# Six local-attention layers written out, with another order of work in each round, other PSUM banks, and another entry to the 8-head attention

## What is computed

```python
x = x + tanh(g_xattn[0]) * L0_xattn(ln(x), ctx)   # 16 heads, keys from 77 context rows
x = x + tanh(g_ffn[0])   * L0_ffn(ln(x), ...)     # six local layers
x = x + tanh(g_xattn[1]) * L1_xattn(ln(x), ctx)   # 8 heads
x = x + tanh(g_ffn[1])   * L1_ffn(ln(x))          # mixture of 8 experts
...                                               # two more pairs

def L0_ffn(x):
    for i in range(6):
        x = attn_layer(shift_tokens(x), Wqkv[i], q_scale[i], k_scale[i], Wo[i]) + x
        x = ffn_layer(shift_tokens(x), ln_g[i], ln_b[i], W1[i], b1[i], W2[i], b2[i]) + x
    return x
```

## Time and profile before

| | us |
|---|---|
| three runs | 2498.87, 2504.11, 2506.43 |
| median | 2504.11 |
| the profiled execution's own time | 2502.32 |
| its span, first to last instruction | 2500.4 |
| mean granted TensorE clock | 0.981 of full |

### The profile page before, as it was taken

The page is one execution under the profiler, slowest core; times in us unless marked ns, Lnnn a source line. Parts: engine busy times, 40 slices in busy tenths (PEclk is TensorE's granted clock), DMA queues, the critical chain, the costliest instruction groups (busy, mean ns, idle before and its releaser), DMA issues. The chain is left out here.

```text
span 2500.4 us, 84963 instructions
## 1 busy us (share of the span) xinstructions
PE 2379.8 (95%) x32650; PEld 1666.1 (67%) x32650; DVE 1861.0 (74%) x4616; ACT 1770.3 (71%) x3859; POOL 1662.9 (67%) x2011
## 2 busy tenths in 40 slices
PE   8889999999999999999999999999889898999898
PEld 6746666566666666566666666666468777999567
DVE  6768887888878887788778878888387776555574
ACT  5668888888878887888878888888653375332555
POOL 5668888888888887788888888888341164000562
PEclk9989999999999999999999999999999998999899
DMA  3011111121111111221121112111350000000022
GB/s 132 2 36 41 34 33 37 48 52 46 32 48 50 47 36 33 55 54 36 34 55 44 48 36 53 33 32 37 89 172 1 1 2 1 1 0 1 20 68 84
DMA packets 98410, 104.07 MB, mean 42 GB/s; under 512 B 34873, under 2 KB 60548, under 8 KB 97540
## 3 DMA queue, kind: packets, MB, share of 16 engines
q1 hardware_dynamic: 98180, 100.93, 15.2%
HBM read 41.31 MB, written 6.09 MB: 19 GB/s over the span
## 5 line engine op out<-in xcount | busy, mean ns | idle before, releaser
L1261 ACT ACTIVATE area<-ps 64x128 f32<-64x128 f32 (+7 forms) x1480 | 747.0, 530 | 201.2 <-PE ps L860 64.8
L1761 POOL TENSOR_TENSOR area<-area 128x512 f32<-128x512 f32 x384 | 485.7, 1275 | 128.5 <-DVE area L2239 120.9
L1776 POOL TENSOR_TENSOR area<-area,rnq 128x512 f32<-128x512 f32 x384 | 397.2, 1045 | 15.3 <-ACT rnq L1434 8.3
L870 PE MATMUL ps<-lw,area 128*128 128x512 f32 x768 | 375.4, 611 | 4.5 <-DVE area L2239 3.2
L898 PE MATMUL ps<-lw,area 128*64 128x512 f32 x1536 | 373.0, 606 | 0.1
L2237 DVE TENSOR_TENSOR area<-ps,table 128x512 f32<-128x512 f32 x384 | 261.3, 681 | 16.9 <-ACT area L1398 16.8
L2219 DVE TENSOR_REDUCE ssq<-area 128x8 f32<-128x512 f32 x384 | 259.6, 676 | 2.1 <-ACT area L1398 2.1
L2239 DVE TENSOR_TENSOR area<-ps,table 128x512 f32<-128x512 f32 x384 | 259.9, 677 | 0.0
L887 PE MATMUL ps<-ident,area 128*128 128x128 f32 x1536 | 237.7, 278 | 5.0 <-POOL area L1776 4.8
L1398 ACT ACTIVATE area<-ps 128x512 f32<-128x512 f32 x384 | 216.8, 590 | 29.3 <-PE ps L870 29.2
L887 PEld LDWEIGHTS ps<-ident,area 128*128 128x128 f32 x1536 | 178.7, 141 | 78.3 <-issue 57.0
(11 more groups left out here) (290 smaller groups left out, 4950.9 us busy)
## 6 DMA issues: line engine op xcount, KB each, us to landing
area<-area SPq DMA_DIRECT2D x768, 64.0 KB, 2.0
lw<-in_wqk SPq DMA_DIRECT2D x24, 256.0 KB
area<-in_moe_w SPq DMA_DIRECT2D x24, 256.0 KB, 2.8
area<-product_rows SPq DMA_DIRECT2D x16, 256.0 KB
moe_gu<-in_wvT SPq DMA_DIRECT2D x12, 256.0 KB, 3.0
moe_gu<-in_wout SPq DMA_DIRECT2D x12, 256.0 KB, 3.0
area<-area SPq DMA_DIRECT2D x96, 31.8 KB
product_rows<-lw SPq DMA_DIRECT2D x7, 308.0 KB
```

What stands on the lines that cost most here:

```text
L870: nc.tensor.matmul(banks[:, lb_qk[j], :], xsT[s], wqk[w.p][:, j * 512:(j + 1) * 512], start=True, stop=True).then_inc(l_qk_ps, 1)
L1261: return nc.scalar.activation(dst, src, ACT.Identity if kw else ACT.Copy, **kw)
L1761: pool.tensor_tensor(QR[s][:, cols], QR[s][:, cols], RA[s][:, cols], ALU.add).then_inc(l_rsum, 1)
L1776: pool.tensor_tensor(rows, rows, rnq[s][:, 8 * j:8 * j + 8, None].to_broadcast([S, 8, LD]), ALU.mult).then_inc(l_qkn, 1)
```

## The change

1. The loops of the local layers are written out in every engine's queue.
2. Each engine has another order in `stages`, with the waits that this order needs; SyncE issues a unit's transfers one letter earlier.
3. The PSUM banks of the passes are others.
4. SyncE's wait for the output weights comes at round 0 and that for the old layer at round 4 of a layer; weights are loaded from round 0 on.
5. `context_weights` is moved ahead of the wait for the last residual (PE) and ahead of the norming into `Y` (ACT).
6. At the end, five groups of value rows are made inside the last two rounds (three, then two) instead of four behind the last but one and one later.
7. In the 8-head attention all layer norms are made in quads ahead of the rounds, into `Y`; the first round (without scores) goes; keys and value rows move by a round; other banks; row groups are read back in three parts (4, 4 and 8 sequences); the wait for all value rows moves from the first scores to the first transpose of probabilities.

Core of the diff, the order of each engine's `stages` shown as it is after:

```diff
-        lb_tokens, lb_qk, lb_qkT, lb_v = 7, (6, 2, 2, 4), (4, 0, 3, 6), (6, 7, 1, 5)
-        lb_scores, lb_probs = ((4, 5), (0, 1)), (0, 6)
-        lb_att, lb_xnT, lb_up, lb_down = 0, 1, (3, 7), 5
-        lb_wvo = (1, 3)
+        lb_tokens, lb_qk, lb_qkT, lb_v = 1, (2, 3, 1, 4), (4, 7, 3, 5), (5, 6, 7, 0)
+        lb_scores, lb_probs = ((3, 4), (6, 7)), (7, 6)
+        lb_att, lb_xnT, lb_up, lb_down = 7, 1, (5, 6), 0
+        lb_wvo = (0, 2)
...
-                with engine.Fori(2, IT - 1) as pr:
+                for pr in range(2, IT - 1):
...
-            with engine.Fori(0, DEPTH // 2 - 1) as lp:
+            for lp in range(DEPTH // 2 - 1):
```

SyncE:

```diff
-                if c: middle_values0(*c)
-                if d: shifted_tokens(*d)
-                if c: middle_values1(*c, edge=edge)
+                if b: middle_values0(*b)
+                if c: shifted_tokens(*c)
+                if b: middle_values1(*b)
...
-                    if n == 3:
+                    if n == 0:
                         sp.wait_ge(l_wvo_ps, 2 * (2 * lp + p + 1))
+                    if n == 4:
                         sp.wait_ge(ffn_done, G + (2 * lp + p) * B)
-                    if 3 <= n < 3 + len(parts):
+                    if n < len(parts):
...
             for i, (lo, hi) in enumerate(RAW):
                 sp.wait_ge(v_ready, 16 + i + 1)
                 rows_to_memory(lo, hi)
+                if i == 2:
+                    sp.wait_ge(rows_out, 16 * FIRST_PIECES)
+                    rows_from_memory(0, 4, rows_in[0])
                 if i == 4:
                     sp.wait_ge(rows_out, 16 * PIECES)
-                    rows_from_memory(0)
+                    rows_from_memory(4, 8, rows_in[1])
```

VectorE, before and after:

```diff
-                if c: first_residual(*c)
                 if a: tokens(*a)
-                if b:
-                    masked(*b, 0)
-                    maxima(*b, 0)
+                if d:
+                    hidden(*d, 0)
+                    hidden(*d, 2)
                 if c:
                     shifted_stats(*c)
                     statistics(*c)
-                if a: rotated(*a, 2)
+                if d: hidden(*d, 1)
+                if a: rotated(*a, 0)
+                if b:
+                    masked(*b, 0)
+                    maxima(*b, 0)
+                    masked(*b, 1)
+                if c: norm_shift(*c)
+                if b: maxima(*b, 1)
+                if a: rotated(*a, 2)
                 if b:
                     sums(*b, 0)
...
                 if d: second_residual(*d, edge=edge)
+                if b: first_residual(*b)
```

Before the local layers and in the attention:

```diff
             strip_attention(XA[0], 0)          (PE)
             pe.wait_ge(w1_loaded, 112)
+            pe.wait_ge(sc_masked, 2 * B)
+            context_weights()
             pe.wait_ge(x_updated, G + LNY)
-            context_weights()
...
             strip_attention(XA[0], 0)          (ACT)
+            context_weights()
             for q in range(QUADS):
                 act.wait_ge(r_shift, q + 1)
                 for c in (2, 3):
                     last = copy(Y[:, q * 4 + c, :], X[:, q * 4 + c, :], scale=RSQ[q][:, c:c + 1], bias=VEQ[q][:, c:c + 1])
                 last.then_inc(x_updated, 2)
             act.wait_ge(v_ones, 4)
-            context_weights()
             for half in range(2):
                 values_outputs(0, 0, half)
```

More of the change, by code:

```diff
@@ L529, in local_transformer @@
             for n in range(B, B + 3):
-                stages(*(layer_unit(1, DEPTH // 2 - 1, n - k) if n - k < B else None for k in range(4)))
-                if drain and n == B + 1: drain()
+                last = tuple(layer_unit(1, DEPTH // 2 - 1, n - k) if n - k < B else None for k in range(4))
+                if drain and n > B:
+                    stages(*last, drained=n - B)
+                else:
+                    stages(*last)
         block = ctx.enter_context(nc.Block())
@@ L708, in first_value_rows, with second_value_rows @@
             def first_value_rows():
-                for i in range(4):
+                for i in range(3):
+                    value_rows(i)
+            def second_value_rows():
+                for i in (3, 4):
                     value_rows(i)
@@ L1038, in quad_T @@
+                if b:
+                    probs_T(*b, 0, ahead=a)
+                    probs_T(*b, 1, ahead=a)
+                if d: down(*d, 1, edge=edge)
+                if c: up(*c, 0)
+                if b:
+                    probs_values(*b, 0)
+                    probs_values(*b, 1)
+                if a: queries_keys_T(*a, 0)
             def quad_T(m, q, banks):
@@ L1245, in _ @@
             pe.wait_ge(t_prep, 1)
[L1246 removed]
+            local_transformer(pe, stages, fresh=True, drain=True)
             attention(XA[1])
```

447 lines of the change are left out of this document (220 added, 227 removed).

## The result

The changed kernel takes 2550.39 us (median of 2545.11, 2549.26, 2551.52 and 2554.05) against 2505.21 for the kernel before: ratio 1.0184, 95% interval 1.0158 to 1.021. It is slower by 45 us, where 2498, a little faster than before, was forecast. The profiled execution took 2545.11, its span 2543.3.

The account below looks back on a forecast made before the run. TensorE hardly rests now; in the new order a loop through VectorE, the shift transfer and GpSimd sets the round. Local layers -8, their entry +3, attention entry -1: -6 on 2502.3 gives 2496; forecast 2498 (median 1.8 higher), range 2446 to 2526.

Parts of the forecast that it names:

- the walk of the new order: Local layers: operation times summed along one round, from the statistics' start to the next, giving 16.73 us a round.
- The loop and its 3.6 us for the shift: Local layers: residual, shift transfer (3.6 us), statistics, rotation, mask and probabilities close a chain that sets the round at 16.73.
- the signs named for it: Local layers: statistics wait for DMA 1 to 2 us a round, TensorE for the mask about 0.4, rounds alternate by 0.3.
- the signs of being wrong: Local layers: rounds of 16.2 with no wait for the mask, or rounds above 17 with waits for GpSimd's probabilities.
- The floor rules: Rival, chance 0.22: the loop is shorter than summed, local-layer rounds fall to 16.2 to 16.4, whole 2446 to 2465.
- The probabilities come later still: Rival, chance 0.26: ScalarE's exponentials or VectorE's reciprocal delay GpSimd's second probabilities in each local-layer round; 0.3 counts, whole 2527.
- Loops and SyncE's wait: Local layers: written-out loops remove 4.1 us once, inner turns nothing; the moved wait removes five disturbances of about 2.5 us.
- Nothing for the longer code: Local layers: written-out loops were charged 0 us for instruction fetches, as queues run ahead of TensorE.
- the third rival: Chance 0.05: the change gives only its removals, the order being neutral; 4 and 12 us go, +2 stays, whole 2490.
- GpSimd's table: Local layers: the next layer's table, six small operations between the two probabilities, lengthens the loop by 5 x 1.4, +7 us.
- Entry of the local layers: Before the first rounds: context-weight copies ahead of ScalarE's normed blocks make the first query product 3 us later; bounds 0, +4.
- Entry of the 8-head attention: After the local layers: keys start 8.7 us earlier, but TensorE waits for group 5's copy; net -1, bounds -9 and +4.

## Why the prediction was wrong, point by point

**The step that failed** is in the walk of the new order: "the second mask follows at 3.30, the shift of the norm at 3.90, the second maximum at 4.02". It gives the shift of the norm 0.1 us. Measured are masks at 1.93 and 3.25 after the statistics, the shift of the norm at 3.85, and the maximum at 4.67. The duration is that of the steady rounds of the kernel before, in which GpSimd was idle or began in nearly the same instant; in the new order GpSimd's differences are running in 95 of 96 rounds when it begins, and in 94 it lasts until they end. The price is 0.69 in a steady round and 0.62 on the average of the local layers, in place of nothing: with 96 rounds 60 us, against a miss of 52. All behind it (probabilities ready at 9.24, found 9.90) is late by this alone.

**The round.** With that operation made short, nothing else changed, the round is 16.65 (forecast 16.73), alternating by 0.3 as forecast, with the statistics waiting for the transfer and TensorE waiting some 0.17 and 0.46 in turn for the mask (23.4 in all); the whole came to 2490 (forecast 2498). The loop and its 3.6 us for the shift (3.75 and 3.45 in turn in the kernel after) were right. So were the signs named for it in the kernel after: waits for the mask (24.4 in 71 times) and for the DMA. And of the signs of being wrong, "rounds above 17 with waits for GpSimd's probabilities" came.

That this run is within 8 us of the forecast is in part luck. Its local layers, measured as in the earlier trace rows, take 1614 (forecast 1619). From the last token transpose to the mixture it is 3.0 more than before, where 1 less was forecast, and the unchanged stages after it are 3.7 shorter, which no term had.

**The rivals.** *The floor rules* needs a shorter loop, which is what the run with GpSimd's order changed has: its floor is 16.36 and not 16.15, since TensorE's pieces summed fell 0.2 short. *The probabilities come later still* had the right place (TensorE waits 19.9 us for them) and the right sign, but its cause was ScalarE's exponential or a reciprocal, half a microsecond at most; both had slack. Its 2527 lies under the result. The range left no room for an operation that itself becomes longer.

**Loops and SyncE's wait.** 4.1 for the turn: 4.2. Nothing for the inner loops, from a wrong reading of the earlier trace rows: 3.6. 5 x 2.5 for the wait: four times, 10.5 together. Nothing for the longer code: TensorE shows 4.4 us of new idle issue in seven places (L937), which is the most that it can have cost; the order of before, written out, does not show it. Both removals were right and are part of the kernel after. The sum of 96 new rounds did not contain them, only the third rival did, so their sizes did not move the forecast. They hide what the new order cost: with both removals the local layers take 1592 in the old order and 1656 in the new one, 64 more, of which the long operation is 59.

**GpSimd's table.** 5 x 1.4 on the chain was forecast; moved away it gave 1.4 or 1.5 a round and 8.7 in all.

**Entry of the local layers.** +3, bounds 0 and +4: in the kernel after the first query product is 5.8 later (139.03 and 133.27), in the four runs with the same entry 3.4 to 5.8; 2.4 is thus the spread between executions of the same code. By the fourth token transpose the five stand at 181.7 to 184.6, where four kernels with the order of before stand at 181.2 to 182.7. So three have made up all of it; the kernel after and one other are still some 2.2 late. The place itself costs 1.6 at the entry and nothing later, as its two runs show. ScalarE's timeline in the kernel after, where the copies of the earlier trace rows now stand ahead of the normed blocks:

```profile
127.61 2.06 ACT L1285 ACTIVATE w<-ps 128x512 f32<-128x512 f32 x4 [10.73 <-PE ps L698]
129.54 3.18 ACT L1285 ACTIVATE Y<-X,m_lg 128x128 f32<-128x128 f32 x8
```

**Entry of the 8-head attention.** The mechanism was right: the value rows stand in the waits before, and TensorE waits behind them for the copy of group 5, 7.06 us (forecast 8 to 10). TensorE's timeline in the kernel after, as in the earlier trace rows:

```profile
1827.00 5.32 PE L714 MATMUL ps<-w,ctxT 128*128 128x512 f32 x12
...
1841.11 6.93 PE L729 MATMUL ps<-ctxT,w 128*128 128x462 f32 x16 [0.60 <-ACT lw L1285]
...
1857.78 2.07 PE L714 MATMUL ps<-w,ctxT 128*128 128x512 f32 x2 [7.06 <-ACT lw L1285]
```

From the last token transpose to the first keys it is 48.8 instead of 52.8, 4 of the 8.7 us; from there to the mixture the gain is gone: 144.8 in all, 142.7 before. -1 was forecast with bounds -9 and +4; +2 came, though the granted clock of this stretch moves it by as much: 142.7 at 0.95 in the kernel before, 138.7 at 0.99 with its loops and wait mended.

## What to carry to other kernels

Before a VectorE operation is moved, ask what GpSimd does at its new place. In these kernels the operation with two tensors from SBUF lasted until the end of the GpSimd operation that had begun shortly before it, and this shows as a longer operation and in no list of waits. For each group of instructions, read the longest duration beside the median: one of eight times the median, in rounds of one kind, is a price that a new order may charge in every round. Where it bites, there are two ways out that worked here: one operand as a pointer scalar, or the operation in GpSimd's pause. One tensor instead of two is no safe rule, as `floors` in the next section shows. And in an order that TensorE nearly fills, check GpSimd's order and VectorE's together.

## What the runs showed of the hardware

**A lock, by who is first.** In 95 of 96 rounds of the kernel after, differences were running when the operation began, as a rule for 0.16 us, and it took 0.90 (median). In the kernel before, 31 of them began 1 to 10 ns behind a GpSimd operation of 1.05 us and took 0.15 all the same; the five that began 76 to 81 ns behind one took 1.21. GpSimd's differences took the same in both kernels (1.04). The other direction, GpSimd held by VectorE, is not shown: the 48 of GpSimd's normalisations in the kernel before that began 0 to 40 ns behind the operation took 1.05 instead of 1.04. Masks and rotations, one operand in PSUM and one in SBUF, ran at 0.68 beside GpSimd throughout. The hidden product, the same kind of instruction as the shift of the norm but with one operand in PSUM, was not held either: 0.35 at the longest of 288. The Trainium skill, "SBUF — State Buffer", section "SBUF: two separate sides", states that VectorE and GpSimd share one pair of ports, held for a whole instruction by whichever starts first, and that a VectorE operation with two SBUF inputs needs it against a GpSimd operation that reads SBUF. The traces agree, with 0.90 and 0.87 against 0.15 and, for the pointer form, 0.20; what they add is that a lead of up to 10 ns did not count.

**Another form is held as well.** `floors` on VectorE has one tensor from SBUF, 128x16, and a constant, and writes the tensor back in place. It takes 0.16 to 0.18 when it is free. In the five rounds of the kernel after that make a table, it began 22 to 35 ns behind GpSimd's second probabilities and took 1.04 to 1.05; VectorE's and GpSimd's timelines:

```profile
371.09 1.05 DVE L2258 TENSOR_SCALAR ssq<-ssq 128x16 f32<-128x16 f32 x1
```

```profile
371.06 1.05 POOL L1820 TENSOR_TENSOR area<-area,rc 128x512 f32<-128x512 f32 x1
```

In the kernel before, 96 of its 192 took 0.31 (median) and ended some 0.03 behind GpSimd's normalisation. It costs nothing there: in the kernel after VectorE waits 0.74 or more for TensorE behind each of the five. But the pointer form of the norm's shift is a `TENSOR_SCALAR` with one tensor too, and was free in 96 of 96 rounds. What separates the two (the constant, the 16 columns, the writing in place) was not run.

**The spread between executions goes with the granted clock after the local layers.** Ten runs of the kernel before with its outer loop written out go from 2484.86 at a mean clock of 0.987 to 2496.29 at 0.982. In the local layers the granted clock is 1.00, and traces with the same code there agree within 1.4 us. Each kernel has one profiled execution, so where the time goes is compared here between two kernels. The windows from the last token transpose to the mixture and from there to the end, same code, of the kernel before:

```profile
1742.20:1884.90 142.70, 121.77 (x884) 82.59 (x881) 82.91 (x223) 83.04 (x166) 53.20 (x63) 0.95 0.40 117
1884.90:2500.40 615.50, 567.36 (x5496) 503.63 (x5494) 393.47 (x1268) 286.43 (x727) 187.11 (x367) 0.95 0.06 18
```

and of the run with SyncE's wait moved:

```profile
1723.10:1861.80 138.70, 117.02 (x891) 78.55 (x881) 82.28 (x220) 82.91 (x166) 53.21 (x63) 0.99 0.41 120
1861.80:2469.60 607.80, 559.98 (x5497) 498.76 (x5495) 392.44 (x1271) 286.21 (x728) 187.09 (x367) 0.97 0.06 18
```

With the same code these stages are 12 us shorter at 0.99 and 0.97 than at 0.95. So a part of a kernel is best judged by its own stretch of the trace, not by the median of the whole. For the kernel after, the two traces give: 4.3 us more before the first token transpose, 45.8 in the local layers, 2.1 from there to the mixture, and 9.3 less in the last stretch (606.2), whose code is unchanged. That makes the 43 by which the span grew.
